# Splitting the left tiles of two key chunks and the turned diagonal tiles into halves for three fp32r products

## The reference, cut to what matters

```
xn = group_norm(x)                              # 32 groups
g  = g_w @ xn + g_b                             # 128 channels
f  = xn^T @ xn                                  # 4096 x 4096 per image
y  = softmax(f, axis=-1) @ g^T                  # per image
out = x + batch_norm(W_w @ y + W_b) + xn
```

## Time and profile before

| what | value |
|---|---|
| median of 3 runs | 2267.2 us (2264.66 to 2268.2) |
| the profiled execution | 2274.37 us, its span 2272.3 us |
| granted TensorE clock, mean | 0.984 |
| PE / DVE / ACT / POOL busy | 94% / 66% / 48% / 36% of the span |

### The profile page before, as it was taken

How to read it: one execution, slowest core, us unless ns; L and a number is a source line. 1 busy time by engine, 2 the same in 40 slices (tenths; PEclk the granted TensorE clock), 3 DMA queues, 4 the chain that set the end, 5 groups by cost and what they waited for, 6 DMA issues and landing times.

```text
span 2272.3 us, 32522 instructions
## 1 busy us (share of the span) xinstructions
PE 2138.1 (94%) x9520; PEld 1522.6 (67%) x9520; DVE 1509.5 (66%) x3062; ACT 1095.2 (48%) x2234; POOL 811.3 (36%) x624
## 2 busy tenths in 40 slices
PE   5899999999999999999999999999999999999988
PEld 4787776665687776665678677665668777666433
DVE  5566666776755766686756666677765676667556
ACT  3344444556444445447444444545644445454645
POOL 3002122559501023347730122345950202345650
PEclk9999999999999999999999999999999999999999
DMA  3112233445512223454521223344551232246879
GB/s 135 75 75 86 95 113 125 163 146 165 181 44 84 100 90 112 144 185 133 192 76 76 79 102 112 125 162 149 174 169 43 88 116 89 93 137 206 304 256 360
DMA packets 108407, 304.55 MB, mean 134 GB/s; under 512 B 11456, under 2 KB 11968, under 8 KB 93888
## 3 DMA queue, kind: packets, MB, share of 16 engines
q1 hardware_dynamic: 108224, 302.37, 38.8%
HBM read 159.71 MB, written 142.61 MB: 133 GB/s over the span
## 4 chain that ended last, share of the span: by engine, by line
PE 67%; POOL 12%; issue 11%; ACT 4%; DVE 3%; DMA 2%; SPq 0%; DVEq 0%; POOLq 0%; ACTq 0%
PE bank L1183 10%; PE bank L1124 10%; PE bank L1126 9%; PE bank L1125 9%; PE bank L1159 8%; POOL fy_d L690 4%; PE bank L1187 4%; PE bank L1189 4%; PE bank L1188 4%; POOL fy_c L690 4%; PE bank L1324 3%; ACT ring L756 2%; PE bank L1254 2%; POOL xl L663 2%; DVE plo L961 1%
## 5 line engine op out<-in xcount | busy, mean ns | idle before, releaser
L782 ACT CAST phi<-bank 128x512 fp32r<-128x512 f32 x480 | 280.6, 586 | 818.8 <-PE bank L1159 818.1
L926 DVE TENSOR_SCALAR_CACHE_REDUCE ring<-bank 128x512 f32<-128x512 f32 x576 | 396.5, 688 | 290.9 <-PE bank L1126 287.4
L1124 PE MATMUL bank<-xh 128*128 128x512 f32 x1152 | 542.0, 471 | 7.2 <-POOL xl L663 6.4
L1126 PE MATMUL bank<-xh,xl 128*128 128x512 f32 x1152 | 457.3, 397 | 0.0
L1125 PE MATMUL bank<-xl,xh 128*128 128x512 f32 x1152 | 454.3, 394 | 0.0
L961 DVE TENSOR_TENSOR plo<-bank,phi 128x512 fp32r<-128x512 f32 x480 | 325.9, 684 | 165.9 <-ACT phi L782 121.8
L1159 PEld LDWEIGHTS bank<-ident,ring 128*128 128x128 f32 x1920 | 234.9, 143 | 201.5 <-issue 131.7
L1159 PE MATMUL bank<-ident,ring 128*128 128x128 f32 x1920 | 296.6, 278 | 60.7 <-ACT ring L756 29.6
L756 ACT ACTIVATE ring<-ring,nmax 128x512 f32<-128x512 f32 x480 | 344.7, 720 | 0.0
L690 POOL TENSOR_TENSOR fy_c<-fy_c,maxrow 128x512 f32<-128x512 f32 x200 | 261.8, 1312 | 159.6 <-DMA fy_c<-spill 159.6
L690 POOL TENSOR_TENSOR fy_d<-fy_d,maxrow 128x512 f32<-128x512 f32 x188 | 241.6, 1288 | 184.0 <-DMA fy_d<-spill 184.0
(11 more groups left out here) (110 smaller groups left out, 2784.0 us busy)
## 6 DMA issues: line engine op xcount, KB each, us to landing
spill<-ring SPq DMA_DIRECT2D x112, 1024.0 KB, 4.4
fy_c<-spill SPq DMA_DIRECT2D x200, 256.0 KB, 4.6
fy_d<-spill SPq DMA_DIRECT2D x188, 256.0 KB, 4.1
ring<-x_dram SPq DMA_DIRECT2D x40, 512.0 KB, 4.6
lbuf<-spill SPq DMA_DIRECT2D x60, 256.0 KB, 3.7
yd<-yn SPq DMA_DIRECT2D x32, 256.0 KB, 3.3
fx_a<-x_dram SPq DMA_DIRECT2D x16, 512.0 KB, 8.3
out_dram<-fx_a SPq DMA_DIRECT2D x16, 512.0 KB, 4.5
```

The lines of the kernel that those rows point to most:

```text
L926: last = nc.vector.tensor_scalar(ring[:, SLOT[u], t, :], src, 1.0, None, ALU.mult, ALU.max, accum_out=rowm[:, t, c:c + 1])
L1124: nc.tensor.matmul(dst, xh[:, k, rows], xh[:, k, cols], start=(k == 0), stop=False)
L1126: last = nc.tensor.matmul(dst, xl[:, k, rows], xh[:, k, cols], start=False, stop=(k == K - 1))
```

## The change

Of the left tiles, those of key chunks 0 and 1 (KEPT = 2) and the turned diagonal tiles now take the way of the split tiles: ACT writes a high half, DVE a low half, and TensorE makes three fp32r products. Left tiles of chunks 2 to 6 stay whole. The rows of gh and gl of chunks 0 and 1 are in use longer and are taken off the buffers for loads, so these are 10 and the one `lbuf`; the rows of the other chunks come free later, after the diagonal tiles. The product of a split left tile waits for its low half and, as before, for its share in the running sum.

```diff
-FULL = range(1, NB)
-SPLIT = [p for p in range(TILES) if not (tile(p)[3] and p // TPB in FULL)]
+KEPT = 2
+def full(p):
+    j, c, _, left = tile(p)
+    return left and KEPT <= c < j
+SPLIT = [p for p in range(TILES) if not full(p)]
...
-SPARE_ROWS = [(h, c) for c in range(NB - 1) for h in range(2)]
-SPARE_FROM = {c: max(p for p in SPLIT if tile(p)[1] == c) + 1 for c in range(NB - 1)}
-SPARE_TO = {c: min([s for s, own in NEXT_G_AT.items() if own == c], default=TILES + 2) for c in range(NB - 1)}
+SPARE_ROWS = [(h, c) for c in range(KEPT, NB - 1) for h in range(2)]
+SPARE_FROM = {c: max(p for p in SPLIT if tile(p)[1] == c) + 1 for c in range(KEPT, NB - 1)}
+SPARE_TO = {c: TILES + 2 for c in range(KEPT, NB - 1)}
...
-                    if c in SPARE_LAST:
-                        used = max([p for p in range(TILES) if tile(p)[1] == c] + [LEFT[SPARE_LAST[c]]])
+                    if c < KEPT:
+                        used = max(p for p in range(TILES) if tile(p)[1] == c)
                         act.wait_ge(tile_used, (b - 1) * TILES + used + 1)
-                        act.wait_ge(left_added, (b - 1) * NLEFT + SPARE_LAST[c] + 1)
...
                 if p in SPLIT_NO:
                     pe.wait_ge(lo_made, b * NSPLIT + SPLIT_NO[p] + 1)
-                else:
+                if left:
                     w = LEFT_NO[p]
```

More of the change, by code:

```diff
@@ L296 @@
            for w in range(NLEFT) if LEFT_BEFORE[w] is not None)
-SPARE_LAST = {c: max(w for w in range(NLEFT) if LEFT_BUF[w] is not None and LEFT_BUF[w] >= LBUFS
-                     and SPARE_ROWS[LEFT_BUF[w] - LBUFS][1] == c) for c in NEXT_G_AT.values()}
 SLOT_USE = [last_use(LAST_IN_SLOT[k]) for k in range(SLOTS)]
```

## The result

The changed kernel takes 2352.8 us in the median (2346.47 to 2357.89), the kernel before 2266.4: a ratio of 1.037 [1.034, 1.040], slower by 86 us. The prediction was 2309 with a range up to 2350: the sign was right, the loss was double the one forecast, and it lies just outside the range. The ratios leave out two executions far off the others, one of early_two (2693.7 us, at a clock of 0.749) and one of the kernel before (5525 us).

The account below looks back on a forecast made before the run. TensorE, VectorE and GpSimd were taken to bound the kernel by place. Stages 1 to 3 -15.2, stage 4 0, stage 5 +23.4 and +3.1, stage 6 +18 and +6, stage 7 +3 and +3.5: +41.8, 2309 us, range 2254 to 2350.

Parts of the forecast that it names:

- The bounds by place: TensorE sets the pace in stages 3, 4 and 7, VectorE in 5, GpSimd in 6 and the last image's 6 and 7.
- Rival 1: Whole kernel: TensorE is the bound all through and covers the rest, -52 us, 2215 us; chance 0.07.
- rival 2: New low halves: two SBUF inputs cost little, coming when GpSimd has just ended; +1, 2268 us; chance 0.16.
- Stage 5: First half: VectorE's work 37.5 us where 30.0 were; +7.8 each in three images, +3.1 in the last.
- the term of the loads: Stages 1 to 3: fewer buffers shorten the loads' lead; charged 0.5 us an image, bounds 0 and 3.
- Stage 6: First half: GpSimd, already full, gets 5.4 us, plus 0.6 for the cast; +6 each in three images, +6 last.
- VectorE's side of a meeting: A subtraction with two SBUF inputs, while GpSimd works, costs VectorE 0.32 us more, bounds 0 and 1.17.
- GpSimd's side: Each meeting costs GpSimd 0.45 us; twelve in stage 6's first half make 5.4 us.
- Stage 4: All images: TensorE 27.7, VectorE 29.1 us, which is the old length; 0, bounds -8 and +12 over four images.
- Stage 7: VectorE 27.5 us against 27.2, +1 each in three images; last image, GpSimd the bound, +3.5.
- Stages 1 to 3: All images: TensorE stays the bound and gains; -3.8 an image, -15.2 over four, bounds -22 and 0.
- Rival 3: Each meeting costs VectorE half a GpSimd operation, 0.64 us; 19 us more in stages 4, 5, 7; 2350 us; chance 0.13.

Follow-up runs that it names:

- early_two: Kernel before with tiles split in stages 1 and 2 alone, all buffers, TensorE waiting for low halves only ahead of the third product: 2255.0 us, ratio 0.994.
- one_input: Changed kernel with the low half of 67 of 76 split left tiles an image subtracting the running sum in PSUM, not the high half: 2302.3 us, ratio 1.016.
- work_only: Kernel before, all buffers, plus one unused VectorE statistics instruction for each left tile that the change splits (76 an image): 2292.2 us, ratio 1.010.
- buffers_only: Kernel before, all left tiles whole, with only the change's 11 buffers: 2274.0 us, ratio 1.003.
- early_stages: Kernel before with the tiles split in stages 1 to 3 alone, all buffers: 2262.8 us, ratio 0.9979.
- the pair: Kernel before with 11 buffers and one added VectorE instruction for 44 tiles an image, with one or two SBUF operands: 2292.5 and 2343.6 us.
- small_from_psum: Changed kernel with split left tiles' low halves over 2 columns, in 67 of 76 an image with the second operand from PSUM: 2262.3 us, ratio 0.998.
- work_two_operands: Kernel before with 11 buffers and an added VectorE maximum with two SBUF operands for 44 left tiles an image: 2343.6 us, ratio 1.034.
- two_cols: Changed kernel with the low halves of split left tiles made over 2 columns instead of 512: 2277.5 us, ratio 1.005.
- work_one_operand: Kernel before with 11 buffers and an added VectorE statistics instruction with one SBUF operand for 44 left tiles an image: 2292.5 us, ratio 1.012.

## Why the prediction came out as it did

- **The bounds by place** were right but for stage 6. TensorE's gain was worth something only in stages 1 and 2; stage 5 was VectorE's; stage 6, given to GpSimd alone, was held by VectorE and GpSimd together. Rival 1 is out. So is rival 2: the new low halves took 0.92 us in the mean, and even with one operand in PSUM (one_input) the time is 2302 where rival 2 had 2268.
- **Stage 5** was forecast at +7.8 for VectorE's work, and work_only, with all buffers, measured +7.5. That near a hit was partly luck: the sum put 1.9 us of meetings into this stage, and there are hardly any (0.70 us for each low half); 28.39 + 7.2 alone would have given +6. The changed kernel's first half grew by 10.0 in the mean; the rest is the term of the loads, which I had charged with 0.5 us an image and put into stages 1 to 3: buffers_only shows +2.4 here.
- **Stage 6 is the step that failed.** It was forecast at +6 in three images and +6 in the last; it became +10.6 and +11.7, some 20 us together (of the 11.7 the fewer buffers alone make 1.8). The term that was mis-sized is VectorE's side of a meeting. I priced it at 0.32 us a tile, the mean of the first sums, and so set VectorE's total of 32.1 us below GpSimd's 35.7. Measured were 1.45 - 0.68 = 0.77 us a tile, and VectorE was busy for 38.72 us. GpSimd's side was priced about right: 19 subtractions start in this half where 16 did, and over three images they average 1.55 us against 1.31, which makes 4.6 us where 5.4 stood. The first sums stand once in a stage, in all stages; the low halves of stage 6 come one after the other while GpSimd is busy for 29.7 of 29.7 us, and 30 of 36 took longer than 0.8 us. My own row for it was 1055.11, 1.08 us, in stage 6; and a mean over the whole run was the wrong one to take.
- **Stage 4** was forecast at 0 and got 3 us in each image, 12 in all: VectorE 30.30 of 31.10, with the low halves at 0.96. Two things were wrong. The old length, 29.7, came from a window 2 us too long. And the price of a meeting, 0.32 us, was halved for GpSimd's share, though the mean of the first sums already holds those that met nothing; measured were 0.96 - 0.68 = 0.28. one_input takes 9 of the 12 us back.
- **Stage 7** went as forecast within a microsecond (+0.4 for +1) in three images; in the last image its first half grew by 5.5 where 3.5 stood, and its second half gave 3.4 back.
- **Stages 1 to 3** seem to have hit: -15.4 for -15.2. That was luck in the main. 9.3 us of it lie in the second half of stage 2, where buffers_only, which splits nothing, is shorter than the profiled run of before by 5.9 as well. Against buffers_only the changed kernel gains 3.0 and 3.2 us over four images in the first halves of stages 1 and 2 and 3.3 in the second half of stage 2, and loses 3.6 in the first half of stage 3: 5.9 in all, under half the forecast. (The second halves of stages 1 and 3 jump by some 3 us from image to image in every kernel.) That a stage among these got longer was to be the sign of late loads; it isn't, as early_stages has it with all buffers.
- **Rival 3** gave 2350 by the price of a half GpSimd operation, 0.64 us, and the time is 2353. Its mechanism was the right one, and its 9 us an image for stage 6 come near the 10.6 measured; of its 19 us for stages 4, 5 and 7, stage 4 shows 12 and stage 5 next to none, so its total is nearer than its parts. This rival deserved more than 0.13. By the Trainium skill, page "SBUF — State Buffer", section "Who interferes with whom", the port pair that the two engines share is an exclusive lock, and a VectorE instruction with two SBUF inputs contends with a GpSimd instruction that reads SBUF. The traces agree: 2.66 us for a low half that started under an operation of 2.37, and 0.68 where the second input comes from PSUM.
- **Taken together**: VectorE's added work 23 us (work_only), the fewer buffers 6 (buffers_only), the second SBUF operand 51 (the pair; 50 by one_input): 80 of the 86. The rest would be what the longer way costs less what TensorE gives back; neither was measured by itself. The parts were measured in different kernels, and each with what the clock did there, so their sum is only a sign that nothing large is missing.
- **The clock** stood in no term of the sum. Its mean fell by 0.012, and in stage 6 of the last image to 0.72. By itself a mean like this doesn't make the loss: at 0.975 an execution of small_from_psum took 2269.5 us and one of work_two_operands 2346.4. But executions of one kernel do get longer with a lower clock (two_cols: 2261.6 us at 0.987, 2286.5 at 0.972), so a part of each difference above may go with it.

## What to carry to other kernels

Before an instruction is added to an engine, read its busy share in the stage where it goes, and read the operands: a VectorE instruction with both inputs in SBUF must be priced against GpSimd's share in that very stage, for both engines, and not by the mean of such instructions elsewhere. Where GpSimd is full, one operand in PSUM, or another place for the instruction, is worth more than its length. And a saving on the engine that is busy most is worth taking only in the stages that this engine holds: split in two of the seven stages, with all buffers kept and with TensorE's later wait, the same tiles make this kernel 0.6% faster (early_two); split in three, without that wait, the gain isn't clear of no change (early_stages).

## What the runs showed of the hardware

- A VectorE instruction needn't be long to meet GpSimd: over 2 columns with two SBUF inputs it took 0.15 us free and up to 1.68 us (two_cols); over 512 columns 0.68 free and up to 2.66 (the changed kernel). With the second input from PSUM the 2-column form never took more than 0.16 us (small_from_psum).
- It works in both directions: of GpSimd's 544 subtractions, 1.28 us in the median, 97 took more than 1.5 us and up to 1.84 beside 176 VectorE instructions with two SBUF inputs (work_two_operands), and 17 beside as many with one (work_one_operand).
- VectorE's statistics over one SBUF tensor show no meeting with GpSimd: all 176 between 671 and 695 ns (work_one_operand), beside a GpSimd that was full.
